# Output projections of a four-layer pair kernel: one block-diagonal matmul, or two half-row matmuls into two banks

## The chip, the cores and the metric

The kernel runs on one core of one Trainium2 chip. The metric is the device time of one execution in microseconds (us). Engines are named as in the profile: PE (TensorE matmul), PEld (TensorE weight load), DVE (VectorE), ACT (ScalarE), POOL (GpSimd), SP (SyncE, here the issuer of most DMAs).

## The reference, cut to what matters

The input is an image x of 192 x 192 tokens with 64 channels, fp32. Four layers are applied one after the other, each as a residual on the group-normalised x:

```
x = x + L0(gn(x)); x = x + L1(gn(x)); x = x + L2(gn(x)); x = x + L3(gn(x))

L0, L1, L3 ("triangle" layers), z = layer_norm(gn(x)):
    left  = (z @ Wl) * sigmoid(z @ Wgl)        # 64 -> 64 channels
    right = (z @ Wr) * sigmoid(z @ Wgr)
    prod[i, j, c] = sum_k left[.., c] * right[.., c]     # per channel, over 192 rows
    y = layer_norm(prod) @ Wo                  # the output projection: 64 -> 64
    result = (y + bo) * sigmoid(z @ Wgo)
L2: an MLP with fp8-like rounding, 64 -> 512 -> 64
```

The change concerns the line `y = layer_norm(prod) @ Wo` of the three triangle layers, and the product with the output gate behind it.

## The kernel before, in words

The tokens lie in 36 tiles (TILES). A tile is 128 partitions by 8 tokens (U) of 64 channels (C), so 128 x 512 numbers. Each engine has its own instruction stream, written out by a helper, `pipeline(eng, stages)`: each stage has a lead, and in turn i the engine does stage f on tile i + lead, in the order of the list. Waits between engines are counting semaphores.

A triangle layer has three stages. The input stage projects every tile; the multiply stage (`multiply`, lines 1121 to 1146) forms the products over 192 rows, per channel; the output stage runs over the 36 tiles again. Only the output stage is touched. Per tile it does, on the engines:

- DVE: layer-norm moments (L671), variance (L680), shift (L687), two of the eight tokens normalised (L698), `gated` (L743: product of the projection in PSUM with the gate), `update` (L750: plus the residual).
- POOL: reciprocal root (L485); in layers 0 and 1 also the shifted copy for the next group norm (L445).
- ACT: six of the eight tokens normalised (L935, six instructions), evacuation of the transposed tile from PSUM to `xnT` (L921); in layers 0 and 1 also the squares (L897).
- PE, in this order: `project_out` of tile t (L1168), `transpose_xn` of tile t + 1 (L1078, four transposes of 128 x 128 into bank 4 or 5), and in layers 0 and 1 `add_to_sums` of tile t - 2 (L1049, two matmuls with a moving operand of 512 columns into banks 6 and 7). In layer 3, the last, there is no `add_to_sums`.
- SP: loads of the residual (L377) and of the gate (L378), store of the result (L388).

An `xnT` buffer holds four blocks of 128 columns (PAIRS = 4). In block k the rows 0 to 63 are the channels of token 2k, the rows 64 to 127 those of token 2k + 1, and the columns are the tile's 128 partitions. The projection of a block uses the block as the stationary operand and a 128 x 128 block-diagonal matrix (`wpair[:, 2 * PROJ:]`, Wo twice on the diagonal) as the moving one. `wfold[:, q, PROJ:]` holds the same Wo, once in the rows 0 to 63 and again in the rows 64 to 127. An fp32 matmul leaves two matmul records and two weight-load records in the trace, and an fp32 transpose one of each, so a tile has 8 records of L1168 and 4 of L1078.

Banks 0 and 1 take the projections (bank b is t mod 2), banks 2 and 3 are not used in this stage. ACT's L921 of tile t waits for the transposes of tile t and for `out_ready` of tile t - 2; PE's L1168 of tile t waits for that L921 and for `prod_ready` of tile t - 2.

Of the kernel before, what the change touches and what calls it, by code (L numbers as in the profile page):

```python
# [23 lines left out]
ALU = mybir.AluOpType  # L24
# [3 lines left out]
P = 128  # L28
N = 192
C = 64  # L30
# [12 lines left out]
PAIRS = U // 2  # L43
# [3 lines left out]
PROJ = 5 * C  # L47
# [53 lines left out]
def wait_free(eng, semaphore, value):  # L101

    if not (isinstance(value, int) and value <= 0):
        eng.wait_ge(semaphore, value)


def build(nc, x_in, weights, biases, norms, mask, mlp_norm, w1, w2, out, layers=4):
    with ExitStack() as ctx:
        def sb(name, shape, dt=F32):
            return ctx.enter_context(nc.sbuf_tensor(name, shape, dt))  # L110
# [13 lines left out]
        def part(buf, lo, n, bufs=2):  # L124
            return buf[:, lo:lo + n * bufs].rearrange("p (b f) -> p b f", b=bufs)


        xin, _, _, xn, xnT = (part(work, 1024 * k, ROW) for k in range(5))
# [5 lines left out]
        wpair = work[:, 10368:10368 + 2 * (PROJ + C)]  # L134
# [3 lines left out]
        xres, gate = part(work, 0, ROW, RING), part(work, 8192, ROW, RING)  # L138
# [26 lines left out]
        wfold = sb("wfold", [P, 3, PROJ + C])  # L165
# [21 lines left out]
        ps = ctx.enter_context(nc.psum_tensor("ps", [P, 8, 512], F32))  # L187
# [60 lines left out]
        def x_base(l):  # L248

            return TILES * l  # L250
# [9 lines left out]
        def tr_base(l, side):  # L260

            return TILES * (2 * TRIANGLES[l] + side)
# [5 lines left out]
        def tile_landed(dmas, l, t, b, ring=2):  # L268


            each = 16 * dmas[l]
            return (t - b) * (each // ring) + (each + all_landed(dmas, l, ring))
# [247 lines left out]
        def _(dve):  # L520
# [218 lines left out]
            def gated(l, t, b, r):  # L739
                q = TRIANGLES[l]  # L740
                dve.wait_ge(out_ready, TILES * q + t + 1)
                dve.wait_ge(res_loaded[r], tile_landed(RES_LOADS, l, t, r, RING))
                dve.tensor_tensor(gate[:, r, :], ps[:, b, :], gate[:, r, :], ALU.mult).then_inc(prod_ready, 1)  # L743

            def update(l, t, b, r):
                dve.wait_ge(prod_ready, x_base(l) + t + 1)
# [112 lines left out]
            for l in range(layers):  # L859
                group_norm(l)  # L860
                dve.wait_ge(gn_ready, l + 1)
                if l in TRIANGLES:
                    q = TRIANGLES[l]
                    pair_weights(q)
                    pipeline(dve, layer_norm(l, 0, xn, 2, [(0, lambda t, b: store_pairs(l, 0, t, b)),
                                                                (0, lambda t, b: store_pairs(l, 1, t, b))]))
                    dve.wait_ge(pair_stored, 2 * TILES * (q + 1))
                    for k in range(BLOCKS):
                        move_products(q, k)
                    dve.wait_ge(z_act, CHANNEL_PAIRS // 2 * BLOCKS * (q + 1))  # L870
                    dve.wait_ge(z_dve, CHANNEL_PAIRS // 2 * BLOCKS * (q + 1))
                    pipeline(dve, layer_norm(l, 1, xn_out, 3, [(0, lambda t, b, r: gated(l, t, b, r), RING),
                                                                (0, lambda t, b, r: update(l, t, b, r), RING)]))
                else:
                    pipeline(dve, layer_norm(l, 0, h_norm, 2, [(0, h_amax), (0, h_scale)]) + [
                                   (1, h_weight),
                                   (0, h_inverse),
                                   (-1, h_add),
                                   (0, h_rescale),
                                   (-1, h_round),  # L880
                                   (5, lambda t, b, r: centre(l, t, b, r), RING)])
                    dve.wait_ge(qT_ready, TILES)
                    pair = lambda pp: (0, lambda t, b, r: hidden_product(pp, t, b, r), RING)
                    round_ = lambda half: (-3, lambda t, b: hidden_round(half, t, b))
                    add = lambda half: (-3, lambda t, b: hidden_add(half, t, b))
                    pipeline(dve, [pair(0), (-6, lambda t, b: mlp_update(l, t, b)),
                                   pair(1), (-1, square_sx), (-1, hidden_amax, RING), add(0), (-1, amax_of_product),
                                   pair(2), round_(0), (-1, hidden_row_scale), add(1), (-1, hidden_inverse),
                                   pair(3), (-1, hidden_rescale), round_(1)])
# [148 lines left out]
        def _(pe):  # L1038
# [15 lines left out]
            for k, (lo, hi) in enumerate(SUM_PARTS):  # L1054
# [4 lines left out]
                if k == 3:  # L1059
# [3 lines left out]
                    for j in range(2):  # L1063
                        last = pe.transpose(ps[:, 3, j * C:(j + 1) * C], wq_y[0:C, 512 + j * P:512 + (j + 1) * P], ident[0:C, 0:C])
# [96 lines left out]
                    main_first_rows(False)  # L1161

            def project_out(l, t, b):
                q = TRIANGLES[l]
                pe.wait_ge(xnT_ready, tr_base(l, 1) + t + 1)
                wait_free(pe, prod_ready, x_base(l) + t - 1)
                for k in range(PAIRS):
                    last = pe.matmul(ps[:, b, k * P:(k + 1) * P], xnT[:, b, k * P:(k + 1) * P],  # L1168
                                     wpair[:, 2 * PROJ:], start=True, stop=True)
                last.then_inc(out_ready, 1)  # L1170

            def transpose_q(t, b):
# [46 lines left out]
            for l in range(layers):  # L1219
                pe.wait_ge(gn_picked, l + 1)  # L1220
                pe.matmul(ps[:, 0, 0:GROUPS], ones[:], gn_roots[:], start=True, stop=True).then_inc(gn_spread, 1)
                if l in TRIANGLES:
                    q = TRIANGLES[l]
                    pe.wait_ge(w_step, q + 2)
                    pipeline(pe, [(0, lambda t, b: project(l, 0, t, b)),
                                  (1, lambda t, b, r: transpose_xn(l, 0, t, b, r), RING),
                                  (0, lambda t, b: project(l, 1, t, b))])
                    for k in range(BLOCKS):
                        multiply(q, k)
                    tail = [] if l == LAST else [(-2, lambda t, b: add_to_sums(t, sum_base(l) + t, b))]  # L1230
                    pipeline(pe, [(0, lambda t, b: project_out(l, t, b)),
                                  (1, lambda t, b, r: transpose_xn(l, 1, t, b, r), RING)] + tail)
                else:
                    pipeline(pe, [(-1, transpose_q)])
                    pair = lambda pp: (0, lambda t, b: hidden_layer(pp, t, b))
                    turn = lambda half: (-4, lambda t, b: transpose_hidden(half, t, b))
                    out_half = lambda half: (-5, lambda t, b: mlp_out(l, half, t, b))
                    sums = lambda bank: (-7, lambda t, b: add_to_sums(t, sum_base(l) + t, b, (bank,)))
                    pipeline(pe, [pair(0), pair(1), sums(SUM), turn(0), out_half(0),
                                  pair(2), sums(SQ), pair(3), turn(1), out_half(1)])  # L1240
# [53 lines left out]
```

## Time and profile before

| | |
|---|---|
| median of 3 runs | 1985.76 us (1978.09 to 1988.72) |
| profiled execution: its time, its span | 1991.03 us, 1989.2 us |
| busy over the span | PE 76%, PEld 49%, DVE 82%, ACT 63%, POOL 52% |
| mean granted TensorE clock | 0.854 of 2.4 GHz |
| output stages, first to last projection | layer 0: 360 to 486 us; layer 1: 780 to 892 us; layer 3: 1876 to 1985 us |

Busy shares are means over stages with different limits, so they say little about one stage. The granted clock is at one of two levels, 0.50 (1.2 GHz) or 1.00 (2.4 GHz); a value between is a mixture over the stretch. Durations of matmul records are latencies and overlap one another: the rate is read from the length of a run of records, less one record, over the number of steps.

### The profile page before, as it was taken

The page shows a single profiled execution, that of the slowest core. Times are in us where ns is not written, and L with a number is a line of the kernel's source. Part 1 is how long each engine was busy: PE and PEld are TensorE (multiplying, and loading weights), DVE is VectorE, ACT ScalarE, POOL GpSimd, SP SyncE. Part 2 cuts the span into 40 slices and gives each one's busy share as a digit, 9 for nine tenths or more (in the row PEclk, how much of TensorE's full clock was granted, in tenths as well). Part 3 has the DMA queues.
Part 4 walks back from the last instruction along what each step waited for, and adds up shares of the span by engine and source line. Part 5 has one row for each costly group of instructions (what it writes and reads, how often), then busy time and mean ns, then how long its engine had stood idle before and what let it go on. Part 6 is the DMA issues. An engine that isn't in the chain of part 4 may idle for free.

```text
span 1989.2 us, 31133 instructions
## 1 busy us (share of the span) xinstructions
PE 1505.3 (76%) x9710; PEld 975.6 (49%) x9744; DVE 1630.4 (82%) x4038; ACT 1251.1 (63%) x2571; POOL 1028.4 (52%) x730
## 2 busy tenths in 40 slices
PE   5479999798799987981111288888888859998775
PEld 1156668564566685650111124444443437776664
DVE  6899961897999717978999958999989979992488
ACT  2256641896455517974566658777787837772488
POOL 7288830685888406867676501222222268870254
PEclk8789999899899998995555558989899889999869
DMA  6034443676344345771111001111111124435377
GB/s 235 11 85 106 107 103 90 182 198 202 85 107 106 81 122 160 212 201 59 38 42 43 22 0 33 43 43 43 43 44 47 50 80 112 111 91 133 104 233 252
DMA packets 314373, 201.96 MB, mean 102 GB/s; under 512 B 248992, under 2 KB 249312, under 8 KB 314208
## 3 DMA queue, kind: packets, MB, share of 16 engines
q1 hardware_dynamic: 175776, 162.21, 28.0%
q10 hardware_dynamic: 138432, 37.76, 8.1%
q8 instruction: 78, 1.28, 0.3%
q14 instruction: 87, 0.71, 0.1%
HBM read 114.97 MB, written 66.06 MB: 91 GB/s over the span
## 4 chain that ended last, share of the span: by engine, by line
issue 37%; PE 28%; DVE 14%; ACT 9%; POOL 6%; DMA 4%; SPq 0%; ACTq 0%; DVEq 0%; POOLq 0%
PE ps L1088 10%; ACT work L935 7%; PE ps L1093 6%; PE ps L1049 4%; PE ps L1078 4%; PE ps L1168 4%; DMA gate_dram<-work 3%; POOL work L445 3%; POOL work L491 2%; DVE stats L671 2%; ACT work L921 2%; DVE ln_s L687 1%; DVE work L592 1%; DVE pairs L789 1%; DVE pairs L757 1%
## 5 line engine op out<-in xcount | busy, mean ns | idle before, releaser
L485 POOL TENSOR_TENSOR ln_s<-ln_s,half_power 128x8 f32<-128x8 f32 x252 | 417.6, 1657 | 373.3 <-DVE ln_s L680 317.4
L1088 PE MATMUL ps<-work 128*128 128x384 f32 x864 | 319.5, 493 | 3.5 <-ACT work L921 3.5
L1049 PE MATMUL ps<-work,ones 128*128 128x512 f32 x504 | 282.3, 677 | 27.0 <-ACT work L897 17.8
L946 ACT ACTIVATE work<-ps 128x768 f32<-128x768 f32 x216 | 175.1, 811 | 175.0 <-DMA gate_dram<-work 141.2
L935 ACT ACTIVATE work<-pairs,ln_s 128x64 f32<-128x64 f32 x648 | 263.0, 493 | 17.8 <-DVE ln_s L687 17.8
L491 POOL TENSOR_TENSOR work<-pairs,work 128x512 f32<-128x512 f32 x36 | 47.5, 1320 | 372.8 <-DVE pairs L855 372.8
L1093 PE MATMUL ps<-work 128*128 128x256 f32 x864 | 223.4, 381 | 0.0
L477 POOL TENSOR_TENSOR work<-work,gn_rstd 128x512 f32<-128x512 f32 x144 | 185.1, 1286 | 62.4 <-DVE work L636 56.9
L1093 PEld LDWEIGHTS ps<-work 128*128 128x128 f32 x864 | 165.7, 192 | 69.6 <-issue 1.8
L1179 PE MATMUL ps<-ident,pairs 128*64 128x128 bf16 x576 | 38.8, 312 | 201.9 <-DVE pairs L789 201.0
L1088 PEld LDWEIGHTS ps<-work 128*128 128x128 f32 x864 | 156.8, 192 | 70.3 <-ACT work L921 6.9
L698 DVE TENSOR_SCALAR work<-work,ln_s 128x64 f32<-128x64 f32 x468 | 187.8, 469 | 0.0
L935 ACT ACTIVATE work<-work,ln_s 128x64 f32<-128x64 f32 x396 | 141.9, 432 | 71.5 <-DVE ln_s L687 71.3
L1078 PE MATMUL ps<-ident,work 128*128 128x128 f32 x864 | 144.7, 294 | 54.5 <-DVE work L698 43.6
L1168 PEld LDWEIGHTS ps<-work 128*128 128x128 f32 x864 | 125.9, 216 | 88.5 <-ACT work L921 56.1
L730 DVE TENSOR_TENSOR pairs<-ps,work 128x512 f32<-128x512 f32 x144 | 151.9, 1055 | 21.1 <-ACT work L946 15.4
L1168 PE MATMUL ps<-work 128*128 128x128 f32 x864 | 136.0, 307 | 42.9 <-ACT work L921 42.9
L445 POOL TENSOR_TENSOR work<-work,anchor 128x512 f32<-128x512 f32 x108 | 139.7, 1294 | 49.4 <-PE ps L1049 38.8
L737 DVE COPY pairs<-ps 128x576 f32<-128x576 f32 x48 | 35.4, 755 | 153.0 <-PE ps L1121 81.2
L985 ACT ACTIVATE pairs<-pairs,rescale 128x256 f32<-128x256 f32 x288 | 122.1, 496 | 52.6 <-DVE work L848 52.6
L1049 PEld LDWEIGHTS ps<-work,ones 128*128 128x128 f32 x504 | 88.1, 202 | 126.0 <-issue 57.6
L921 ACT ACTIVATE work<-ps 128x512 f32<-128x512 f32 x216 | 128.2, 594 | 33.7 <-PE ps L1078 32.0
(131 smaller groups left out, 3189.5 us busy)
## 6 DMA issues: line engine op xcount, KB each, us to landing
work<-x_mid SPq DMA_DIRECT2D x144, 256.0 KB, 2.7
gate_dram<-work ACTq DMA_DIRECT2D x108, 256.0 KB, 3.1
work<-gate_dram SPq DMA_DIRECT2D x108, 256.0 KB, 3.1
work<-in_x_in SPq DMA_DIRECT2D x72, 256.0 KB, 2.8
work<-x_nat SPq DMA_DIRECT2D x144, 128.0 KB, 3.0
x_mid<-work SPq DMA_DIRECT2D x72, 256.0 KB, 2.1
work<-pairs SPq DMA_DIRECT2D x96, 96.0 KB, 3.0
work<-pairs ACTq DMA_DIRECT2D x96, 96.0 KB, 3.1
```

Of the source, the lines that this page charges most:

```text
L445: pool.tensor_tensor(tokens(shifted[:, b, :]), tokens(src), over_tokens(anchor[:]), ALU.subtract)\
L477: pool.tensor_tensor(tokens(normed[:, r, :]), tokens(normed[:, r, :]), over_tokens(gn_rstd[:]), ALU.mult)\
L485: pool.tensor_tensor(ln_s[:, b, RSTD, :], ln_s[:, b, VAR, :], half_power[:, 0:U], ALU.pow)\
L698: last = dve.tensor_scalar(dst[:, r % dst.shape[1], u * C:(u + 1) * C], src(u), small(b, RSTD)[:, u:u + 1], small(b, SHIFT)[:, u:u + 1], A ...
L921: act.activation(xnT[:, b, :], ps[:, T_BANK + b, :], ACT.Copy, bias=1.0 / ROOT_C).then_inc(xnT_ready, 1)
L935: last = act.activation(dst[:, r % dst.shape[1], u * C:(u + 1) * C], src, ACT.Identity, scale=ln_s[:, b, RSTD, u:u + 1], bias=ln_s[:, b, S ...
L946: act.activation(sig[:, b, :].rearrange("p (k g) -> p k g", k=PAIRS)[:, 2 * half:2 * half + 2, :], ps[:, bank:bank + 2, 0:GATES], ACT.Sigm ...
L1049: last = pe.matmul(ps[:, bank, :], ones[:], src[:, b, :], start=first, stop=end, skip_group_check=True)
L1078: last = pe.transpose(ps[:, T_BANK + b, k * P:(k + 1) * P], src[:, k * P:(k + 1) * P], ident[:])
L1088: last = pe.matmul(ps[:, GATE_BANK[half] + k, 0:GATES], xnT[:, b, (2 * half + k) * P:(2 * half + k + 1) * P], wpair[:, VALUES:VALUES + GAT ...
L1093: last = pe.matmul(ps[:, half, k * VALUES:(k + 1) * VALUES], xnT[:, b, (2 * half + k) * P:(2 * half + k + 1) * P], wpair[:, 0:VALUES], sta ...
L1168: last = pe.matmul(ps[:, b, k * P:(k + 1) * P], xnT[:, b, k * P:(k + 1) * P], wpair[:, 2 * PROJ:], start=True, stop=True)
```

## The change: what it does

Every block's projection becomes two matmuls. Each takes 64 of the 128 rows: the rows 0 to 63 (even token) against `wfold[0:64]` into bank 2b, the rows 64 to 127 (odd token) against `wfold[64:128]` into bank 2b + 1. The moving operand has 64 columns in place of 128, and the stationary one still has 128. Even tokens of a tile now lie in one bank and odd ones in another, so `gated` reads both banks in one instruction, with an access pattern that puts them back in order. The block-diagonal part of `wpair` is still written.

```diff
@@ gated (DVE)
-                dve.tensor_tensor(gate[:, r, :], ps[:, b, :], gate[:, r, :], ALU.mult).then_inc(prod_ready, 1)
+                by_parity = gate[:, r, :].rearrange("p (k e c) -> p e k c", k=PAIRS, e=2)
+                dve.tensor_tensor(by_parity, ps[:, 2 * b:2 * b + 2, 0:PAIRS * C].rearrange("p e (k c) -> p e k c", k=PAIRS), by_parity,
+                                  ALU.mult).then_inc(prod_ready, 1)
@@ project_out (PE)
                 for k in range(PAIRS):
-                    last = pe.matmul(ps[:, b, k * P:(k + 1) * P], xnT[:, b, k * P:(k + 1) * P],
-                                     wpair[:, 2 * PROJ:], start=True, stop=True)
+                    for odd in range(2):
+                        rows = slice(C * odd, C * odd + C)
+                        last = pe.matmul(ps[:, 2 * b + odd, k * C:(k + 1) * C], xnT[rows, b, k * P:(k + 1) * P],
+                                         wfold[rows, q, PROJ:PROJ + C], start=True, stop=True)
                 last.then_inc(out_ready, 1)
```

## Rows read from the trace of the kernel before

**Rows 1.** The page: busy time by engine; granted clock in 40 slices.

```profile
PE 1505.3 (76%) x9710; PEld 975.6 (49%) x9744; DVE 1630.4 (82%) x4038; ACT 1251.1 (63%) x2571; POOL 1028.4 (52%) x730
...
PEclk8789999899899998995555558989899889999869
```

**Rows 2.** Timeline, layer 0's output stage: start, length, engine, line, records.

```profile
402.46 1.98 PE L1049 MATMUL ps<-work,ones 128*128 128x512 f32 x4
...
404.28 1.05 PE L1168 MATMUL ps<-work 128*128 128x128 f32 x8
...
405.17 0.60 PE L1078 MATMUL ps<-ident,work 128*128 128x128 f32 x4
405.29 0.61 ACT L897 ACTIVATE work<-work 128x512 f32<-128x512 f32 x1
...
405.81 0.59 ACT L921 ACTIVATE work<-ps 128x512 f32<-128x512 f32 x1
...
406.30 2.44 ACT L935 ACTIVATE work<-pairs,ln_s 128x64 f32<-128x64 f32 x6
...
408.64 0.61 ACT L897 ACTIVATE work<-work 128x512 f32<-128x512 f32 x1
...
409.31 1.98 PE L1049 MATMUL ps<-work,ones 128*128 128x512 f32 x4
```

**Rows 3.** Timeline of PE, projections alone: layer 0, then layer 3.

```profile
380.35 1.05 PE L1168 MATMUL ps<-work 128*128 128x128 f32 x8
...
482.28 1.05 PE L1168 MATMUL ps<-work 128*128 128x128 f32 x8
...
1875.74 2.08 PE L1168 MATMUL ps<-work 128*128 128x128 f32 x8 [1.66 <-ACT work L921]
...
1984.06 1.16 PE L1168 MATMUL ps<-work 128*128 128x128 f32 x8 [0.69 <-ACT work L921]
```

**Rows 4.** Timeline, layer 3, around the rise of the clock.

```profile
1919.11 2.08 PE L1168 MATMUL ps<-work 128*128 128x128 f32 x8 [0.69 <-ACT work L921]
...
1920.97 1.06 PE L1078 MATMUL ps<-ident,work 128*128 128x128 f32 x4
...
1922.07 0.60 ACT L921 ACTIVATE work<-ps 128x512 f32<-128x512 f32 x1 [0.70 <-PE ps L1078]
...
1922.72 1.16 PE L1168 MATMUL ps<-work 128*128 128x128 f32 x8 [0.69 <-ACT work L921]
...
1923.72 0.60 PE L1078 MATMUL ps<-ident,work 128*128 128x128 f32 x4
...
1924.90 0.57 ACT L921 ACTIVATE work<-ps 128x512 f32<-128x512 f32 x1
```

**Rows 5.** Windows: length, busy us by engine (records), clock, DMA share, GB/s.

```profile
1872.00:1920.50 48.50, 37.61 (x154) 32.42 (x155) 36.63 (x138) 40.02 (x98) 23.08 (x15) 0.50 0.59 196
1922.00:1987.00 65.00, 36.29 (x273) 30.82 (x272) 58.28 (x204) 60.26 (x149) 34.84 (x20) 0.99 0.79 260
```

**Rows 6.** By line: weight loads, duration ns min/median/max.

```profile
L1168 PEld LDWEIGHTS ps<-work x864: 186/192/338, 360.3 to 1984.8; 128*128 128x128 f32 x173
...
L1131 PEld LDWEIGHTS ps<-work x384: 182/187/335, 295.9 to 1860.8; 64*128 64x128 f32 x192
...
L1146 PEld LDWEIGHTS ps<-work x768: 129/133/228, 295.1 to 1861.8; 64*64 64x64 f32 x192
```

**Rows 7.** Timeline of PE in the multiply stage of layer 0 (rows*columns loaded).

```profile
309.09 5.47 PE L1121 MATMUL ps<-pairs 128*128 128x192 f32 x32
...
315.95 0.89 PE L1146 MATMUL ps<-work 64*64 64x96 f32 x32
316.77 3.09 PE L1131 MATMUL ps<-work 64*128 64x192 f32 x32
319.80 0.89 PE L1146 MATMUL ps<-work 64*64 64x96 f32 x32
```

**Rows 8.** By line, 316.7 to 316.9 us: first matmuls after a change of shape.

```profile
L1131 PE MATMUL ps<-work x2: 427/427/427, 316.8 to 316.8; 64*128 64x192 f32 x2
```

**Rows 9.** Timeline of PE, layer 2: full and 64-row matmuls in turn.

```profile
1203.28 0.39 PE L1195 MATMUL ps<-w1s,pairs 64*128 64x512 bf16 x1
1203.60 0.39 PE L1194 MATMUL ps<-w1s,pairs 128*128 128x512 bf16 x1
...
1205.16 0.86 PE L1213 MATMUL ps<-w2s,work 128*128 128x64 bf16 x24
```

**Rows 10.** By line: DVE reading one bank (L743) and two banks (L802).

```profile
L743 DVE TENSOR_TENSOR work<-ps,work x108: 675/682/694, 362.4 to 1985.3; 128x512 f32<-128x512 f32 x108
...
L802 DVE TENSOR_TENSOR pairs<-ps,pairs x144: 629/679/693, 1149.1 to 1571.8; 128x512 f32<-128x512 f32 x144
```

## The prediction, made before the changed kernel was run

> **What bounds the kernel now.** I read the page first. No engine is full over the whole span, and the granted clock sits at its lower level in several slices [rows 1], so I went by stage. The change touches three stretches only, the output stages, and there I looked at the timeline.
>
> In layer 0's output stage [rows 2] two engines hand one chain to and fro. The evacuation L921 at 405.81 follows the last transpose (405.17 + 0.60 = 405.77). Then ACT does its six normalisations, and L897 at 408.64; PE's sums start at 409.31, when L897 has ended (409.25). From there the same order follows as from 402.46: L1168 1.82 us after the sums' start, L1078 0.89 us after that, L921 0.64 us later. Once round is 0.49 + 2.34 + 0.67 + 1.82 + 0.89 + 0.64 = 6.85 us, and it carries two tiles: 3.43 us a tile. Twenty intervals from 380.35 and seven more up to 482.28 [rows 3] have that pace (3.35 and 3.50 in turn); between them lies one refill of the loads. So a microsecond more in L1168 costs half a microsecond a tile. A microsecond less would bring little: ACT's own starts add up to 0.49 + 2.34 + 0.52 = 3.35 us a tile (L897 to L921 is 0.52 at 405.29), so 0.08 us is all there is. Layer 1 is the same.
>
> Layer 3 has no sums, and two regimes [rows 4]. Up to 1922 the clock is 0.50 [rows 5], and L921, L1168, L1078 of the next tile and its L921 form a closed ring with nothing beside it: 0.65 + 1.86 + 1.10 = 3.61 us a tile. From 1922 on the clock is 1.00, L1078 ends at 1924.32 and ACT comes to L921 only at 1924.90: ACT is the bound, 2.81 us a tile, and PE has 0.58 us of slack. The stage's 35 intervals take 1984.06 - 1875.74 = 108.3 us [rows 3], 13 of them at 3.61.
>
> **The change part by part.**
>
> The gating product on DVE has the same 128 x 512 elements. Another product that reads two banks takes 679 ns, against 682 for this one with one bank [rows 10]; runs of 64 elements stay whole. Nothing. Bounds: 0 to 0.05 us a tile, behind slack in layers 0 and 1, and at most 23 x 0.05 = 1.2 us in layer 3. No wait is added: banks 2 and 3 are free here, `out_ready` and `prod_ready` count as before, and no DMA moves. PE's records of L1168 double to 16 a tile; L1146 sends 32 in 0.89 us [rows 7], so issue is not the limit.
>
> The projection itself. Do two 64-row matmuls run side by side? L1131 does just this, with 192 columns: 32 records in 3.09 us, (3.09 - 0.32) / 31 = 89 ns a record, against (5.47 - 0.33) / 31 = 166 ns for L1121 on all rows [rows 7]. Yes, in pairs. So sixteen records of 64 columns would stream in a quarter of that width: 64 columns take 0.055 us, and eight pairs 0.44 us, where eight records at (1.05 - 0.275) / 7 = 0.111 us took 0.89 us [rows 2]. But each record needs its own weight load of 128 columns. A load of 64 rows by 128 columns takes 187 ns, one of 128 rows by 128 columns 192, one of 64 by 64 133 [rows 6]: the duration goes with columns, not rows, 54 ns for 64 of them, so 0.108 us of occupation for 128. A load overlaps the matmul of the same rows, but the next one can't go in before that matmul has started. The pace of a pair is then the longer of 0.108 and 0.055: about 0.11 us, the pace of a single record today. Eight pairs take the 0.89 us that eight records took. I take no gain in the stream, apart from the last record, which is half as wide: -0.055 us. The other bound is the full halving (0.44 us), which is a rival below.
>
> The Trainium skill says the same of loads ("TensorE: Matmul & The Clock Gate", LDWEIGHTS section: a load of 32 rows takes as long as one of 128, only columns count). [rows 6] agree.
>
> The change of shape. PE now goes from full matmuls (L1049) to 64-row ones and back to full transposes, twice a tile. L1146 to L1131: the last L1146 starts at 316.84 - 0.24 = 316.60, streams some 0.08, and L1131 starts at 316.77, 0.09 late; and its first matmuls take 427 ns and not 322 [rows 7, 8], since their load isn't hidden: 0.105 more. L1131 to L1146: last start 319.86 - 0.32 = 319.54, plus 0.16 of streaming, next at 319.80: 0.10 us. In layer 2, 512 columns of bf16 on 128 and 64 rows in turn come every 0.32 us, where 64 columns take (0.86 - 0.20) / 23 = 0.029 us, so 512 about 0.22: 0.10 us a change [rows 9]. I take entry at 0.09 + 0.105 = 0.20 us and exit at 0.09 + 0.055 = 0.145 us (a transpose's load is shorter). Before, both places cost nothing: L1078 follows L1168 at the pace of 0.11. The sum at 2.4 GHz is 0.20 - 0.055 + 0.145 = +0.29 us a tile. Bounds: 0.10 - 0.055 + 0.10 = 0.145, and 0.24 - 0.04 + 0.20 = 0.40 (a pair that starts askew, as L1131's 89 ns in place of 80 hints).
>
> The Trainium skill ("TensorEngine Tiling (Array Packing)", Key Properties) states that changing the mode drains the engine. The trace agrees, at 0.09 to 0.10 us of empty array each time.
>
> In layers 0 and 1: 27 intervals x 0.29 / 2 = 3.9 us, about three intervals at the ends where PE alone is the bound 0.9, three slow ones at the start 0.3, say 5.3 us a layer, 10.6 for both (5.5 to 14.5).
>
> In layer 3 at 1.2 GHz: the wait for L921 empties the array and leaves the first load bare already today, so entry costs nothing. Stream end: -0.11. Exit: about 0.13 + 0.07 = +0.20. Ring: 3.61 + 0.09 = 3.70 us (3.66 to 3.81). At 2.4 GHz the 0.29 us lie in the slack of 0.58.
>
> **The clock.** In layer 3 it stayed at 1.2 GHz for 48.5 us with PE busy 78% by the records, and rose at 1922 with nothing in the order of the work changed [rows 4, 5]. That is a stretch on the edge. The change halves the array's streaming time in the larger group of matmuls there, with loads taking its place, and makes the tile a little longer. I expect that the clock then doesn't rise before the end. The 35 intervals take 35 x 3.70 = 129.5 us, not 108.3: +21.2 us. That is the largest term. In layers 0 and 1 the wide sums keep the engine streaming, and the clock should stay up.
>
> Sum: 10.6 + 21.2 = +31.8 us on the profiled execution's 1991.03 (span 1989.2 and 1.8 around it), so 2022.8. That execution lies 5.3 us above the median of the three runs; on the median it is 1985.8 + 31.8 = 2017.6, forecast **2018 us**.
>
> **Rivals.**
>
> *The clock rises as before.* All else the same, layer 3 costs 13 x 0.09 = 1.2 us and the total is +11.8: 1997.6 us. For it: loads don't shrink, and if they count, the engine is as active as ever; and at 2.4 GHz PE was only 56% busy for 65 us and didn't fall [rows 5]. Against: the late rise.
>
> *No cost for changing shape.* Then layers 0 and 1 get 54 x 0.055 / 2 = 1.5 us less, layer 3's slow ring 13 x 0.11 = 1.4 us less: 1983 us, and 1997 if the clock stays down. Against: all four changes in [rows 7] and the pace in [rows 9].
>
> *The stream is halved after all: faster.* If a 64-row load occupied its half for 0.055 us only (decides below about 0.08 us a pair), L1168 would be 0.44 us shorter and with the changes of shape 0.1 shorter net. Layers 0 and 1 could give at most 54 x 0.08 = 4.3 us, up to ACT's 3.35. In layer 3's slow ring 8 x 0.1 = 0.8 us go and 0.2 come: 3.0 us a tile, at either clock near ACT's 2.81. The stage takes 35 x 2.9 = 101.5, -6.8 us. Total -11: 1975 us. Against: the 187 ns of the 64-row load. The Trainium skill ("TensorEngine Tiling (Array Packing)", Theoretical Speedup: up to 2x where a dimension is 64 or less) speaks for this rival.
>
> **How the numbers follow.** Forecast 0.60, clock rises 0.20, no cost of shape 0.08, halved stream 0.12. The forecast's own range, from its bounds (5.5 to 14.5; 35 x 3.66 to 3.81) with some 5 us for the spread of the runs, is 2008 to 2031. The range over cases, 1986 to 2031, leaves out the halved stream and part of the one before it. A measurement of this kernel can tell about 0.5%, here 9.9 us, from no change. Slower: the forecast, two thirds of the second case, a little of the third: 0.74. Faster: most of the fourth: 0.11. The rest, 0.15, is within.
>
> **What would show it.** Right: L1168 has 16 records in about 0.95 to 1.05 us at clock 1.00, the first ones longer than the rest by 0.1; L1078 starts 1.0 us after L1168, not 0.89, and L1168 0.2 us later behind the sums; the tile of layer 0 takes 3.57 us, in turns of about 3.65 and 3.50; layer 3's windows show 0.50 to the end and a tile of 3.70 us; L743 stays at 0.68. Wrong: pairs every 0.06 us; L1168 right behind L1049; or a layer 3 that reaches 1.00 and stays there. What would make the total wrong most easily is the clock, with 20 us on it.

## The result, and the profile after

The changed kernel takes 2023.6 us (median of 4 runs, 2015.35 to 2026.17), against 1986.2 us for the kernel before on the same chip: a ratio of 1.0188, interval 1.0147 to 1.0230, so 29 to 46 us more. The forecast was 2018, +32 us. The profiled execution has a span of 2021.9 us, 32.7 more than before.

The page of the kernel after, busy time and granted clock:

```profile
PE 1553.0 (77%) x10574; PEld 998.8 (49%) x10608; DVE 1637.6 (81%) x4038; ACT 1253.1 (62%) x2571; POOL 1026.1 (51%) x730
...
PEclk8789999899899998995555559899898989999655
```

The totals barely move, but the last slices of PEclk do: 9 8 6 9 before [rows 1], 9 6 5 5 now. That is layer 3's output stage.

The timeline of layer 0's output stage after (L1051, L1080, L923, L937 and L899 are the L1049, L1078, L921, L935 and L897 of before):

```profile
402.90 1.11 PE L1173 MATMUL ps<-wfold,work 64*128 64x64 f32 x16
...
403.94 0.66 PE L1080 MATMUL ps<-ident,work 128*128 128x128 f32 x4
...
404.43 1.90 PE L1051 MATMUL ps<-work,ones 128*128 128x512 f32 x4
...
404.63 0.60 ACT L923 ACTIVATE work<-ps 128x512 f32<-128x512 f32 x1 [0.34 <-PE ps L1080]
...
406.26 1.11 PE L1173 MATMUL ps<-wfold,work 64*128 64x64 f32 x16
...
408.15 1.98 PE L1051 MATMUL ps<-work,ones 128*128 128x512 f32 x4 [0.20 <-ACT work L899]
...
410.06 1.11 PE L1173 MATMUL ps<-wfold,work 64*128 64x64 f32 x16
```

Read it against [rows 2]. Twice the records take 1.11 us in place of 1.05, so nothing was won in the stream. From the projection's start to L1080's start it is 403.94 - 402.90 = 1.04 us, before 0.89. From there to the evacuation 0.69, before 0.64. And from the sums' start at 408.15 to the projection it is 1.91 us, before 1.82. Together 0.15 + 0.05 + 0.09 = 0.29 us a tile. Two tiles take 410.06 - 402.90 = 7.16 us in place of 6.85, the tiles in turns of 3.36 and 3.80. The 0.34 us in brackets is new: ACT now waits for PE's transposes once in two tiles.

Layer 3, the same kernel: timeline, then a window (columns as in [rows 5]).

```profile
1886.39 1.97 PE L1173 MATMUL ps<-wfold,work 64*128 64x64 f32 x16 [1.66 <-ACT work L923]
...
1952.99 1.97 PE L1173 MATMUL ps<-wfold,work 64*128 64x64 f32 x16 [0.69 <-ACT work L923]
1954.89 1.11 PE L1080 MATMUL ps<-ident,work 128*128 128x128 f32 x4
...
1956.05 0.60 ACT L923 ACTIVATE work<-ps 128x512 f32<-128x512 f32 x1 [0.80 <-PE ps L1080]
...
1956.69 1.97 PE L1173 MATMUL ps<-wfold,work 64*128 64x64 f32 x16 [0.69 <-ACT work L923]
```
```profile
1890.00:2010.00 120.00, 97.93 (x654) 81.36 (x656) 87.86 (x316) 94.50 (x230) 51.18 (x32) 0.50 0.64 213
```

The ring is 3.70 us a tile from the first to the last, the clock never leaves 0.50, and PE is busy 82% of the time by its records, more than the 78% of before [rows 5]. The last projection starts at 2015.89, so the stage's 35 intervals take 129.5 us, before 108.3.

From the first projection to the last, in the profiled executions (us):

| | layer 0 | layer 1 | layer 3 |
|---|---|---|---|
| before | 125.0 | 127.3 | 108.3 |
| after | 129.0 | 133.9 | 129.5 |
| difference | +4.0 | +6.6 | +21.2 |

That is 31.8 of the 32.7 us. (Layer 1's stage before the change ran from 764 to 891 us, not from 780.)

Layer 1's +6.6 isn't the array's work alone. In both kernels one load of the gate is late there (`gated` waits 4.1 us for it before and 4.3 after), PE then stands idle for over 3 us, and the clock falls for a moment, for twice as long after the change. Windows of layer 1, before and then after:

```profile
861.10:864.50 3.40, 3.40 (x7) 1.61 (x6) 2.46 (x10) 2.87 (x8) 1.65 (x2) 0.50 1.09 299
```
```profile
871.50:878.30 6.80, 6.80 (x26) 3.73 (x25) 4.41 (x18) 4.37 (x12) 3.53 (x3) 0.50 1.07 277
```

The 21 intervals ahead of this gap take 3.0 us more than before, in layer 0 as well; the eight behind it 3.4 us more in layer 1, and 1.2 in layer 0, where no such fall stands in either profile.

The gating product all but keeps its duration, 690 ns in the median (before 682, [rows 10]):

```profile
L744 DVE TENSOR_TENSOR work<-ps,work x108: 675/690/692, 363.4 to 2017.9; 128x512 f32<-128x512 f32 x108
```

### The profile page after: what moved, and what is told of

It is laid out like the page before. It is cut to its first block, busy times and chain, and to the rows that moved or that the text cites. A ratio compares the mean times of both kernels' runs of the same rounds, so it can differ in the third digit from the quotient of the medians.

```text
span 2021.9 us, 32861 instructions
## 1 busy us (share of the span) xinstructions
PE 1553.0 (77%) x10574; PEld 998.8 (49%) x10608; DVE 1637.6 (81%) x4038; ACT 1253.1 (62%) x2571; POOL 1026.1 (51%) x730
## 4 chain that ended last, share of the span: by engine, by line
issue 38%; PE 27%; DVE 20%; POOL 6%; ACT 4%; DMA 4%; SPq 0%; DVEq 0%; ACTq 0%; POOLq 0%
PE ps L1090 9%; PE ps L1095 6%; PE ps L1173 5%; PE ps L1080 5%; DVE stats L671 3%; DMA gate_dram<-work 3%; DVE work L698 3%; POOL work L445 2%; POOL work L491 2%; PE ps L1051 2%; ACT work L937 2%; ACT work L923 2%; DVE ln_s L687 1%; DVE work L752 1%; DVE work L592 1%
## 5 line engine op out<-in xcount | busy, mean ns | idle before, releaser
L1051 PE MATMUL ps<-work,ones 128*128 128x512 f32 x504 | 279.5, 671 | 24.7 <-ACT work L899 15.7
L937 ACT ACTIVATE work<-pairs,ln_s 128x64 f32<-128x64 f32 x648 | 261.9, 487 | 16.9 <-DVE ln_s L687 16.9
L1080 PE MATMUL ps<-ident,work 128*128 128x128 f32 x864 | 161.3, 316 | 54.5 <-DVE work L698 43.2
L1095 PEld LDWEIGHTS ps<-work 128*128 128x128 f32 x864 | 165.8, 192 | 69.5 <-issue 1.8
L1090 PEld LDWEIGHTS ps<-work 128*128 128x128 f32 x864 | 157.3, 193 | 69.6 <-ACT work L923 6.0
L1173 PEld LDWEIGHTS ps<-wfold,work 64*128 64x128 f32 x1728 | 139.8, 242 | 99.9 <-issue 51.3
L937 ACT ACTIVATE work<-work,ln_s 128x64 f32<-128x64 f32 x396 | 142.0, 432 | 71.5 <-DVE ln_s L687 71.3
L1173 PE MATMUL ps<-wfold,work 64*128 64x64 f32 x1728 | 156.8, 336 | 31.7 <-ACT work L923 31.7
L923 ACT ACTIVATE work<-ps 128x512 f32<-128x512 f32 x216 | 128.2, 593 | 64.2 <-PE ps L1080 64.1
L1080 PEld LDWEIGHTS ps<-ident,work 128*128 128x128 f32 x864 | 108.8, 158 | 89.7 <-DVE work L698 42.7
```

What stands on the lines that cost most here:

```text
L923: act.activation(xnT[:, b, :], ps[:, T_BANK + b, :], ACT.Copy, bias=1.0 / ROOT_C).then_inc(xnT_ready, 1)
L937: last = act.activation(dst[:, r % dst.shape[1], u * C:(u + 1) * C], src, ACT.Identity, scale=ln_s[:, b, RSTD, u:u + 1], bias=ln_s[:, b, S ...
L1051: last = pe.matmul(ps[:, bank, :], ones[:], src[:, b, :], start=first, stop=end, skip_group_check=True)
L1080: last = pe.transpose(ps[:, T_BANK + b, k * P:(k + 1) * P], src[:, k * P:(k + 1) * P], ident[:])
L1090: last = pe.matmul(ps[:, GATE_BANK[half] + k, 0:GATES], xnT[:, b, (2 * half + k) * P:(2 * half + k + 1) * P], wpair[:, VALUES:VALUES + GAT ...
L1095: last = pe.matmul(ps[:, half, k * VALUES:(k + 1) * VALUES], xnT[:, b, (2 * half + k) * P:(2 * half + k + 1) * P], wpair[:, 0:VALUES], sta ...
```

## The experiments

Twelve kernels ran. Ratios are to the kernel before on the same chip, whose medians there were 1988.5 (one stage at a time, and the idle matmul alone), 1991.4 (the gating part, half the columns, one extra matmul or pair) and 1991.0 (the four with a burst). Half the columns and the two extra ones are single executions, read for their timelines and not for their totals of 1977.0, 1989.4 and 1999.3 us.

### One stage at a time

The 64-row form in layer 3 alone, and in layers 0 and 1 alone:

```diff
# rows_layer3 (rows_layers01: l != LAST), in gated and in project_out
+                if l == LAST:
+                    ... the changed kernel's lines
+                else:
+                    ... the lines of before
```

> 64-row projections in layer 3 alone, layers 0 and 1 as before. Theory (in layer 3 the price is the clock that stays at 1.2 GHz, since the halved streaming keeps it down): layer 3's 35 intervals take 35 x 3.70 = 129.5 us instead of 108.3, clock 0.50 to the end, total +21 to +23 us, about 2008. Rival (the clock's rise in layer 3 is a matter of where the stage happens to begin, and the 64-row form has no part in it): the clock rises during the stage, 2.81 us a tile from there, total within 5 us of before.

Measured: 2013.5 us, ratio 1.0124 (1.0100 to 1.0148), +20 to +29 us. Projections from 1875.73 to 2005.24: 129.5 us, clock 0.50 throughout:

```profile
1890.00:2000.00 110.00, 89.54 (x597) 74.38 (x598) 80.24 (x288) 86.96 (x210) 46.76 (x29) 0.50 0.63 211
```

In the profiled execution the stage starts at the very time at which it started before (1875.74, [rows 3]), so where the stage lies isn't what keeps the clock down. The rival falls.

> 64-row projections in layers 0 and 1 alone, layer 3 as before. Theory (two changes of array shape a tile, 0.29 us together, half of it on the ring of ACT and PE): 3.57 us a tile instead of 3.43, total +10 to +13 us, about 1998, layer 3 with its clock rising part of the way through as before. Rival (layer 3's clock depends on what came long before): layer 3 stays at 0.50 here too, total +30 us or more.

Measured: 1995.4 us, ratio 1.0039 (1.0020 to 1.0058), +4 to +12 us, mostly less than the expected +10 to +13. The profiled execution is the slowest of the ten (2004.7 us). Layer 0 takes 132.2 and layer 1 132.0 us in the profiled execution, in turns of 3.36 and 3.80 as in the changed kernel. Layer 3 is 108.35 us long, as before, with the clock rising after 13 tiles, although it starts 13.6 us later:

```profile
1890.00:1935.00 45.00, 36.76 (x153) 31.95 (x153) 33.67 (x123) 36.49 (x89) 20.28 (x13) 0.50 0.61 201
1937.00:1995.00 58.00, 32.82 (x249) 27.82 (x247) 53.80 (x196) 58.00 (x146) 33.68 (x19) 1.00 0.84 276
```

The two parts add up, 0.4% and 1.2% to the 1.9% of the whole, within the intervals. The rise comes after 13 tiles in this profile as in that of before, and after 14 in that of the next run, so its place in the stage is fairly steady.

### The gating part alone

```diff
-                    last = pe.matmul(ps[:, b, k * P:(k + 1) * P], xnT...
+                    last = pe.matmul(ps[:, 2 * b + k // 2, k % 2 * P:(k % 2 + 1) * P], xnT...
-                dve.tensor_tensor(gate[:, r, :], ps[:, b, :], gate[:, r, :], ALU.mult)
+                halves = gate[:, r, :].rearrange("p (h f) -> p h f", h=2)
+                dve.tensor_tensor(halves, ps[:, 2 * b:2 * b + 2, 0:2 * P], halves, ALU.mult)
```

> Full 128-row block-diagonal projections as before, but blocks 0 and 1 of a tile go to bank 2b and blocks 2 and 3 to bank 2b + 1, and the gating product reads both banks. Theory (the gating part of the change costs nothing): the product stays at 0.68 to 0.69 us, layer 0 125 to 127 us and layer 3 108.3 us from first to last projection, total within 0.3% of before. Rival (two banks, or the wider access pattern, take part in the loss): more than 5 us slower.

Measured: ratio 1.0000 (0.9987 to 1.0012), the product at 684 ns, stages of 125.3, 127.3 and 109.1 us. Two banks cost nothing that these runs can tell (0.1%). The interleaving by parity wasn't tried alone; in the changed kernel it comes with 690 ns.

### What sets the pace of the stream

```diff
-                        last = pe.matmul(ps[:, 2 * b + odd, ...], xnT[rows, b, k * P:(k + 1) * P],
+                        last = pe.matmul(ps[0:C, 2 * b + odd, ...], xnT[rows, b, k * P:k * P + C],
```

> The changed kernel with stationary blocks of 64 columns in place of 128, so only the partitions 0 to 63 of each tile are projected; the other half of the output is left out. Theory (the weight load sets the pace of a pair, 0.108 us for 128 columns): a pair every 0.055 to 0.06 us, the 16 records of a tile take 0.65 to 0.75 us at 2.4 GHz in place of 1.11. Rival (the matmul itself or the issue of four instructions a pair sets it): still 1.11 us, as the moving operand and the number of instructions are the same.

Measured: the 16 records of a tile take 0.68 us at 2.4 GHz, and 1.12 at 1.2 GHz where they took 1.97. Timeline of layers 0 and 3:

```profile
403.21 0.68 PE L1173 MATMUL ps<-wfold,work 64*64 64x64 f32 x16
403.82 0.66 PE L1080 MATMUL ps<-ident,work 128*128 128x128 f32 x4
```
```profile
1941.58 1.12 PE L1173 MATMUL ps<-wfold,work 64*64 64x64 f32 x16 [0.69 <-ACT work L923]
1942.62 1.11 PE L1080 MATMUL ps<-ident,work 128*128 128x128 f32 x4
...
1943.77 0.60 ACT L923 ACTIVATE work<-ps 128x512 f32<-128x512 f32 x1
...
1944.42 1.12 PE L1173 MATMUL ps<-wfold,work 64*64 64x64 f32 x16 [0.69 <-ACT work L923]
```

The moving operand and the number of instructions are those of the changed kernel; the columns loaded are halved, and with them the output partitions written. The start of the second pair is 0.05 us late here as in the changed kernel, and then a pair comes every (0.68 - 0.22 - 0.05) / 7, about 0.06 us, not 0.11. The rival falls: neither the moving operand nor the issue set the pace. Whether it is the load or the output partitions these runs can't tell apart, since the two go together; the load's duration is known to follow the columns [rows 6]. The Trainium skill's rule that a load's time goes with its columns, whatever its rows ("TensorE: Matmul & The Clock Gate", LDWEIGHTS section), holds here, and the speedup of up to 2x of the Trainium skill's "TensorEngine Tiling (Array Packing)", Theoretical Speedup, isn't reached by the change: 1.11 us against 1.05. With this short a burst layer 3 runs at 2.84 us a tile (1941.58 to 1944.42) at 1.2 GHz, close to ACT's pace. So it is the length of the burst that makes the low clock dear.

### What a change of shape costs

```diff
# extra_full, behind each tile's projection
+                pe.matmul(ps[:, 2, 0:C], xnT[:, b, 0:P], wfold[:, q, PROJ:PROJ + C], start=True, stop=True)
# extra_rows, in its place
+                for odd in range(2):
+                    rows = slice(C * odd, C * odd + C)
+                    pe.matmul(ps[:, 2 + odd, 0:C], xnT[rows, b, 0:P], wfold[rows, q, PROJ:PROJ + C], start=True, stop=True)
```

> The kernel before plus, behind each tile's projection, one more 128-row matmul with a moving operand of 64 columns into bank 2, which nothing reads. Both theories: two more records at the pace of a load, so L1078 starts 0.89 + 0.22 = 1.11 us after the projection at 2.4 GHz, 3.5 us a tile in layers 0 and 1. It is the yardstick for the next run.

> The kernel before plus, behind each tile's projection, the same work as one pair of 64-row matmuls into banks 2 and 3, which nothing reads. Theory (a change of array shape costs 0.2 us in and 0.145 us out): the transposes start 1.11 + 0.29 = 1.40 us after the projection's start at 2.4 GHz, 3.66 to 3.7 us a tile in layers 0 and 1. Rival (no cost of the change of shape): 1.11 us, as in the run with one full matmul.

Measured, timeline of layer 0, extra_full and then extra_rows:

```profile
401.23 1.05 PE L1168 MATMUL ps<-work 128*128 128x128 f32 x8
402.12 0.33 PE L1171 MATMUL ps<-wfold,work 128*128 128x64 f32 x2
402.29 0.61 PE L1078 MATMUL ps<-ident,work 128*128 128x128 f32 x4
```
```profile
404.40 1.05 PE L1168 MATMUL ps<-work 128*128 128x128 f32 x8
405.38 0.44 PE L1173 MATMUL ps<-wfold,work 64*128 64x64 f32 x4
405.75 0.66 PE L1078 MATMUL ps<-ident,work 128*128 128x128 f32 x4
```

From the projection's start to the transposes' it is 1.06 us with the full matmul and 1.35 with the pair. Both are 0.05 under what was expected: in extra_full the second record of the extra matmul follows the first by 0.06 us and not by 0.11. The difference is the 0.29 us expected. The transposes themselves take another 0.05 us longer (0.66 against 0.61), so going into the 64-row shape and back costs 0.34 us in all, where the prediction had 0.20 + 0.145 = 0.345. In the changed kernel some 0.055 us of that comes back, as its last pair is half as wide as the record in its place before, which leaves the 0.29 of the stages. The tiles agree: 3.51 us in layers 0 and 1 with the full matmul and 3.68 with the pair, as expected, half of 0.34 apart. The rival (no cost) falls.

### What the clock does in layer 3

An idle matmul of 256 columns behind layer 3's transposes, first in the changed kernel and then in the one before:

```diff
+            def keep_streaming(t, b):
+                pe.matmul(ps[:, SUM, 0:2 * P], ones[:], wfold[:, 0, 0:2 * P], start=True, stop=True)
...
+                    keep = [(1, keep_streaming)] if l == LAST else []
                     pipeline(pe, [(0, lambda t, b: project_out(l, t, b)),
-                                  (1, lambda t, b, r: transpose_xn(l, 1, t, b, r), RING)] + tail)
+                                  (1, lambda t, b, r: transpose_xn(l, 1, t, b, r), RING)] + keep + tail)
```

> The changed kernel plus one fp32 matmul of 256 columns a tile behind layer 3's transposes, into bank 6, which nothing reads; it streams while PE waits for the evacuation. Theory (the clock in layer 3 is down for lack of streaming): the clock rises within some 10 us of the stage's start and stays, 2.81 to 2.9 us a tile in layer 3, so 35 x 2.85 = 100 us against 129.5, total about 2023 - 29 = 1994. Rival (something else holds the clock or the pace): it stays at 0.50 and 3.70 us or more a tile, 2023 or above.

Measured: 2028.0 us, ratio 1.0195 (1.0174 to 1.0216). The expectation failed. Layer 3 runs at 3.80 us a tile with the clock at 0.50 to the end, though PE is busy without a break by its records:

```profile
1884.00:2020.00 136.00, 135.20 (x787) 107.86 (x786) 94.22 (x333) 100.41 (x242) 54.16 (x34) 0.50 0.57 192
```

So a PE that is never idle isn't enough to raise the clock.

> The kernel before plus the same idle matmul behind layer 3's transposes. Theory: the clock rises early, 2.81 us a tile in nearly all of layer 3 (98 to 101 us against 108.3), total -7 to -10 us, about 1978. Rival (the filler gets in the way of the projection or evacuation at either clock, or the clock does not follow): 1986 or above.

Measured: 1983.1 us, ratio 0.9979 (0.9966 to 0.9993), 1 to 7 us faster, less than the 7 to 10 expected. The same matmul beside the block-diagonal projections brings the clock up within the first tiles, and layer 3 takes 98.9 us:

```profile
1870.00:1880.00 10.00, 4.78 (x19) 4.09 (x20) 6.23 (x31) 7.53 (x19) 6.91 (x5) 0.60 0.53 182
1880.00:1890.00 10.00, 8.18 (x51) 6.43 (x51) 9.43 (x35) 9.86 (x25) 5.54 (x4) 0.89 0.60 210
1890.00:1900.00 10.00, 7.45 (x53) 5.84 (x51) 9.25 (x36) 10.00 (x27) 6.17 (x4) 1.00 0.84 283
```

The two kernels with one extra matmul or pair bear on this too. Timeline of layer 3 in extra_rows:

```profile
1890.49 2.08 PE L1168 MATMUL ps<-work 128*128 128x128 f32 x8 [1.66 <-ACT work L921]
1892.49 0.69 PE L1173 MATMUL ps<-wfold,work 64*128 64x64 f32 x4
...
1894.92 2.08 PE L1168 MATMUL ps<-work 128*128 128x128 f32 x8 [0.69 <-ACT work L921]
...
1899.35 1.16 PE L1168 MATMUL ps<-work 128*128 128x128 f32 x8 [0.69 <-ACT work L921]
1900.44 0.44 PE L1173 MATMUL ps<-wfold,work 64*128 64x64 f32 x4
```

The clock rises after two tiles and stays up, though each tile has a 64-row pair and both changes of shape; in extra_full it rises after six, and before after 13. So neither 64-row matmuls nor changes of shape keep the clock down by themselves, as far as these single executions go. What keeps it down is that 64-row matmuls stand in place of the full projections.

Then a burst ahead of each output stage, while PE waits 6.6 us for the first normalised tile, with and without the idle matmul:

```diff
+                    pe.wait_ge(z_act, CHANNEL_PAIRS // 2 * BLOCKS * (q + 1) - 1)
+                    for _ in range(7):
+                        pe.matmul(ps[:, 0, :], ones[:], wfold[:].rearrange("p q e -> p (q e)")[:, 0:512], start=True, stop=True)
```

> The changed kernel plus the same burst. It tells whether the 64-row form only fails to bring the clock up, or can't hold it either. Theory (halved streaming also fails to hold it at ACT's pace): the clock falls soon after layer 3's stage begins, 120 to 130 us from first to last projection. Rival (it would hold what it has): 98 to 100 us in layer 3, and a total within 3 us of the kernel before.

Measured: 2017.9 us, ratio 1.0145 (1.0120 to 1.0170). The 64-row form can't hold the clock. It falls after a single tile:

```profile
1879.54 1.11 PE L1173 MATMUL ps<-wfold,work 64*128 64x64 f32 x16 [2.13 <-ACT work L923]
1880.58 0.99 PE L1080 MATMUL ps<-ident,work 128*128 128x128 f32 x4
1882.36 1.97 PE L1173 MATMUL ps<-wfold,work 64*128 64x64 f32 x16 [0.79 <-ACT work L923]
```

> The kernel before plus seven fp32 matmuls of 512 columns into bank 0, which nothing reads, in each triangle layer between the multiply stage and the output stage, where PE waits 6.6 us for the first normalised tile. Theory (the clock is lost in that wait, and at 2.4 GHz the block-diagonal form holds it): clock 1.00 from the first tile on, layer 3 at 2.81 us a tile, 98 to 99 us from first to last projection against 108.3, layers 0 and 1 2 to 4 us shorter each, total -12 to -16 us, about 1975. Rival (the burst delays the first tile, or the clock falls all the same): within 4 us of before.

Measured: 1985.7 us, ratio 0.9979 (0.9960 to 0.9997), less than expected. In the profiled execution the clock is 1.00 throughout layer 3, which takes 98.4 us (1876.17 to 1974.56). But the ten executions have mean clocks of 0.872 to 0.873 (three, 1977.9 to 1981.7 us) and of 0.855 to 0.861 (seven, 1982.8 to 1992.4 us). Layers 0 and 1 weren't 2 to 4 us shorter, as expected, but take 126.2 and 127.1 us, as before. The means suggest that the clock is up in layer 3 in three executions and not, or not all the way, in the seven, which have no trace. Whether it fell there or the burst never raised it is open.

> The kernel before plus the burst and the idle matmul of 256 columns a tile in layer 3. Theory: nothing over the burst alone, since the clock is up already: 98 to 99 us in layer 3, about 1975. Rival (the burst alone does not hold the clock): 98 to 99 us here and more in the run with the burst alone.

Measured: 1978.4 us, ratio 0.9939 (0.9919 to 0.9959), 8 to 16 us faster than before, mean clock 0.866 to 0.873 in all six. With the idle matmul no execution falls behind, against the theory that it adds nothing. This is the fastest version that computes the whole output, and it leaves the projections as they were. The burst alone isn't dependable: in layer 0 of this profile the first two tiles take 3.62 us each, the pace of 1.2 GHz. Its window:

```profile
1876.00:1975.00 99.00, 70.23 (x485) 56.32 (x484) 90.86 (x325) 94.72 (x234) 56.27 (x32) 1.00 0.79 264
```

> The changed kernel plus the burst and the idle matmul in layer 3. Theory: with the clock up from the start, the idle matmul holds it: 98 to 100 us in layer 3, and what is left of the change is its shape changes in layers 0 and 1, so some 10 us above the kernel before with the same two additions. Rival (the 64-row form lowers the clock whatever streams beside it, as the run with the idle matmul alone could suggest): 129 to 133 us in layer 3.

Measured: two groups of five executions, 1985.3 to 1990.4 us with mean clocks of 0.868 to 0.870, and 2018.3 to 2022.2 us with 0.836 to 0.839. The ratio of 0.9985 (0.9961 to 1.0009) compares the first group only. The profile is of that group, and has layer 3 at 98.5 us with the clock up:

```profile
1884.00:1985.00 101.00, 75.64 (x786) 59.09 (x786) 92.06 (x331) 96.81 (x240) 57.70 (x33) 1.00 0.78 259
```

The first group is what the theory said, its median 9.9 us above that of the kernel before with the same two additions. The second group has no trace. Its numbers are those of the rival: the step of some 31 us is that of layer 3 at 1.2 GHz (129 to 133 against 98.5), and 0.032 of mean clock is 2 x 0.032 x 2000 = 128 us more at half speed, as long as that stage. So the 64-row form next to an idle matmul seems to be at the edge here.

## Why the prediction was right

**The stream gains nothing: right.** Eight pairs at the pace of a load. 16 records take 1.11 us, and 0.68 with half the columns loaded.

**Two changes of shape, 0.29 us a tile: right in sum.** The stages show 0.15 + 0.05 + 0.09, and the run with one extra pair 0.34 over its yardstick, against 0.345 before the narrower last pair is taken off. The split was off: the first pair's matmuls wait about 0.05 us for their load and not 0.105 (their records take 321 ns, the others 272, and the next pair comes later by as much), and the way out is dearer by that amount.

**Half of it on the ring of ACT and PE: right.** 7.16 us for two tiles over 16 intervals (388.59 to 445.83), forecast 7.14, before 6.85. The turns were forecast at 3.65 and 3.50 and are 3.36 and 3.80: PE's delay falls wholly on one parity, where ACT's slack of the other doesn't help. Layers 0 and 1 were to cost 10.6 us and cost 4.0 + 6.6. That the sum agrees to the tenth is luck. The prediction's terms for a layer, 3.9 + 0.9 + 0.3, add up to 5.1 and not to the 5.3 that it goes on with. The two long gaps between tiles, which it left out, were 0.7 us shorter in layer 0. And the clock, which it said should stay up there, was down for 6.8 us in layer 1 where it had been for 3.4, and that makes up for it. In the run with those layers alone it was 7.2 + 4.7 in the profile and 4 to 12 in the timing.

**Layer 3 stays at 1.2 GHz: right.** +21.2 us forecast, +21.2 measured. The ring at low clock was 3.70 as forecast. That the 64-row form is what keeps the clock down is shown: that form alone in layer 3 does it, it drops a clock that a burst had raised, and an idle matmul next to it doesn't raise the clock where the same one does beside full-width projections. The reason given for it, the halved streaming, fits these runs and extra_rows, where the full projections stay and the clock rises. It wasn't tested by itself, and what exactly the chip counts was not settled. The +21.2 also rests on the profiled execution before, in which the clock rose after 13 tiles.

**The sum.** Forecast +31.8, profile +32.7, medians +37 (29 to 46). The remaining 0.9 us in the spans is the last tile, drained at the low clock: 6.0 us from the last projection to the end, before 5.1.

**The rivals.** "The clock rises as before" would have been about the effect of rows_layers01, 7 us by the medians, where its own sum was 11.8. "No cost of changing shape" falls with extra_rows. (Its time with the clock down should read 1998.5 and not 1997: 35 x 3.50 - 108.3 - 1.5 = 12.7 us on 1985.8, an estimate from the same rows.) "The stream is halved" needs loads of half the columns; with them it happened.

**Left open.** Layer 3 was 9.4 us shorter with the idle matmul in the kernel before, but the timing gave only 1 to 7 us. The executions of the kernel before spread over 15 us on one chip and their mean clocks over 0.849 to 0.862, so some of them may raise the clock in layer 3 earlier than the profiled one; they have no trace to show it.

## What to carry to other kernels

Splitting a block-diagonal matmul into row tiles halves the streaming, not the weight loads: with as many columns loaded as streamed, or more, look at the load's duration by columns before expecting anything. Count two changes of array shape a turn (0.34 us here) wherever row tiles alternate with full matmuls on a path that matters. And where PE isn't the bound, look at the granted clock as well: a "more efficient" form can cost the clock, and then PE becomes the bound; idle matmuls in PE's waits can be worth more than shorter ones.

## What the runs showed of the hardware that was not expected

- The granted clock doesn't follow PE's busy share. It stayed at 0.50 with PE busy 135.2 of 136.0 us (64-row projections, transposes and an idle matmul), and at 0.99 with PE busy 56% (the kernel before, [rows 5]).
- The same program on the same chip can give two times: ten executions of one kernel gave 1985 to 1990 and 2018 to 2022 us, five of each. The median of such a kernel says little; the mean clock of each execution tells the groups apart.
- Two 64-row tiles load their weights side by side: sixteen loads of 128 columns a tile fit into 1.11 us, where eight loads of full height took 1.05.
